# Value block 7 ahead of the scores, four PSUM banks for the last outputs, and a new order for the first tiles of the feed-forward part

## The reference

```python
x = x + tanh(g_xattn) * attention(layernorm(x), ctx, ctx)
x = x + tanh(g_ffn) * ffn(layernorm(x))
```

## Time and profile before

| | us |
|---|---|
| median of 3 runs | 1479.5 |
| the runs | 1479.43 to 1481.12 |
| the profiled execution, its own time | 1474.84 |
| its span in the trace | 1472.9 |

### The profile page before, as it was taken

One profiled execution on the slowest core, in us unless ns is written; L12 is line 12 of the kernel. 1 busy time (PEld: TensorE's weight loads), 2 busy tenths in 40 slices (PEclk: granted clock), 3 DMA queues, 4 the chain that ended last, 5 costly groups with the idle time before them and its releaser, 6 DMA issues.

```text
span 1472.9 us, 19153 instructions
## 1 busy us (share of the span) xinstructions
PE 1424.6 (97%) x7235; PEld 1167.6 (79%) x7248; DVE 1002.9 (68%) x1565; ACT 564.4 (38%) x865; POOL 614.9 (42%) x429
## 2 busy tenths in 40 slices
PE   7999999999999999999999999999999999998887
PEld 7888888888888888887878888888888888874443
DVE  5866675757576766667475757666566667578997
ACT  4424241414142323234542423232232324148995
POOL 3455242434343343441343433434333424243884
PEclk9999999999999999999999999999999999999999
DMA  8834243433425243437265242333343424455565
GB/s 289 264 98 114 78 109 72 109 80 94 102 69 120 65 107 81 104 85 215 95 186 138 68 104 67 92 83 88 86 95 76 106 65 109 85 170 196 129 130 100
DMA packets 327131, 166.52 MB, mean 113 GB/s; under 512 B 275200, under 2 KB 290048, under 8 KB 326656
## 3 DMA queue, kind: packets, MB, share of 16 engines
q1 hardware_dynamic: 324448, 154.29, 39.4%
q0 software_dynamic: 2592, 11.01, 4.5%
HBM read 132.74 MB, written 35.65 MB: 114 GB/s over the span
## 4 chain that ended last, share of the span: by engine, by line
PE 78%; DVE 12%; DMA 3%; issue 2%; POOL 2%; ACT 2%; SPq 1%; POOLq 0%; ACTq 0%; DVEq 0%
PE psum L569 16%; PE psum L571 16%; PE psum L570 16%; PE psum L623 8%; PE psum L658 8%; PE psum L660 7%; PE psum L659 7%; DVE psum L1638 2%; DVE vw_lo L1368 1%; DVE res L1685 1%; DMA acc<-in_x 1%; DMA wv_raw<-in_wv_t 1%; SPq L368 1%; DVE xg L1648 1%; POOL rot L1253 1%
## 5 line engine op out<-in xcount | busy, mean ns | idle before, releaser
L569 PE MATMUL psum<-xt_hi,wq_hi 128*128 128x512 f32 x1024 | 400.9, 391 | 1.5 <-DVE xt_lo L1368 1.5
L571 PE MATMUL psum<-xt_hi,wq_lo 128*128 128x512 f32 x1024 | 398.6, 389 | 0.0
L570 PE MATMUL psum<-xt_lo,wq_hi 128*128 128x512 f32 x1024 | 398.5, 389 | 0.0
L1225 POOL TENSOR_TENSOR wq_lo<-wq_raw,wq_hi 128x512 fp32r<-128x512 f32 x128 | 170.0, 1340 | 484.3 <-ACT wq_hi L932 484.0
L1529 DVE TENSOR_TENSOR acc<-psum,acc 128x512 f32<-128x512 f32 x224 | 151.4, 681 | 140.0 <-PE psum L660 140.0
L1253 POOL TENSOR_TENSOR rot<-rot 128x1024 f32<-128x1024 f32 x64 | 153.6, 2400 | 207.8 <-DVE rot L1472 207.0
L978 ACT ACTIVATE vw_hi<-psum 64x512 fp32r<-64x512 f32 x256 | 151.7, 593 | 191.6 <-PE psum L571 187.9
L569 PEld LDWEIGHTS psum<-xt_hi,wq_hi 128*128 128x128 f32 x1024 | 192.3, 188 | 40.8 <-DVE xt_lo L1368 1.7
L571 PEld LDWEIGHTS psum<-xt_hi,wq_lo 128*128 128x128 f32 x1024 | 192.2, 188 | 40.1
L570 PEld LDWEIGHTS psum<-xt_lo,wq_hi 128*128 128x128 f32 x1024 | 192.4, 188 | 39.2
L1368 DVE TENSOR_TENSOR vw_lo<-psum,vw_hi 64x512 fp32r<-64x512 f32 x256 | 175.5, 687 | 53.9 <-ACT vw_hi L978 47.7
(11 more groups left out here) (153 smaller groups left out, 1910.0 us busy)
## 6 DMA issues: line engine op xcount, KB each, us to landing
wq_raw<-in_wq_t SPq DMA_DIRECT2D x128, 256.0 KB, 4.4
wd_raw<-in_wd_t SPq DMA_DIRECT2D x128, 256.0 KB, 3.7
p_scratch<-prob SPq DMA_DIRECT2D x60, 256.0 KB, 2.0
pt_raw<-p_scratch SPq DMA_DIRECT2D x240, 64.0 KB, 2.5
acc<-in_x SPq DMA_DIRECT2D x16, 512.0 KB, 5.3
out_x<-acc SPq DMA_DIRECT2D x16, 512.0 KB, 4.7
xa<-out_x SPq DMA_DIRECT2D x16, 512.0 KB, 3.6
out_x<-res POOLq DMA_DIRECT2D x15, 512.0 KB, 5.5
```

Of the source, the lines that this page charges most:

```text
L569: pe.matmul(dst, a_hi, b_hi, start=start, stop=False)
L570: pe.matmul(dst, a_hi, b_lo, start=False, stop=False)
L571: return pe.matmul(dst, a_lo, b_hi, start=False, stop=stop)
L1225: pool.tensor_tensor(dst, full, hi.bitcast(F32), ALU.subtract).then_inc(done, 1)
```

## The change

It consists of these parts:

- In `slot` on TensorE, kind 0, filled: `values(gg - 1, 7)` stands ahead of `score(unit - 1)`.
- In the last group of the second half, the outputs from the fifth on use banks 4 to 7 in turn (`out_bank`), on TensorE and in VectorE's `add`. From output 6 on, the wait for adds is for four outputs back; output 6 waits for all `vw_lo`. `gate(0)` and `up(0)` wait for the adds of outputs 12 and 13 (before: 14 and 15), and `turn_inter(0)` waits for all.
- ScalarE's `last_outputs(1)`: `rows(2)` comes between the evacuations of tile 0, `silu(0)` ahead of `evacuate_gate(1)`, one deviation less stands ahead of `evacuate_gate(1)`; the deviations of the last two tiles are done in steps 2 and 3 of the loop.
- VectorE: the copy of the gate's factors stands between the adds of outputs 11 and 12, and tile 2's `scale_gate`, `gate_greatest` and `scales`, with `up_rows(0)` in between, come at the end of `last_outputs(1)`; the loop begins a step later.

```diff
--- before.py
+++ after.py
@@ -318,6 +318,12 @@
                 n, t = c % 2, (c - 2 * BT) // 2
             return b, n, t
 
+        def out_bank(gg, c):
+
+            if gg == HALVES * GROUPS - 1 and c >= 4:
+                return bank(O_BANK + c % 4)
+            return bank(O_BANK + c % 2)
+
         gate_scales = bank(2, 2)[:, P:DIM]
         small_scales = bank(2)[:, 0:16].rearrange("p (k n) -> p k n", k=2)
 
@@ -650,9 +656,14 @@
                     pe.wait_ge(pt_lo_done, gg * UPG + HB + b + 1)
                 if c % BT == 0:
                     pe.wait_ge(vw_lo_done, 2 * (gg * VPG + 4 * ((c // BT) % 2) + 4))
-                if gg * OPG + c >= 2:
+                four = gg == HALVES * GROUPS - 1 and c >= 6
+                if four and c == 6:
+                    pe.wait_ge(vw_lo_done, 2 * (gg * VPG + VPG))
+                if four and c >= 8:
+                    pe.wait_ge(o_done, gg * OPG + c - 3)
+                if not four and gg * OPG + c >= 2:
                     pe.wait_ge(o_done, gg * OPG + c - 1)
-                cols, dst = slice(n * CH, (n + 1) * CH), bank(O_BANK + c % 2)
+                cols, dst = slice(n * CH, (n + 1) * CH), out_bank(gg, c)
                 for p in range(2):
                     p_hi, p_lo = pt_hi[:, p, b, t * P:(t + 1) * P], pt_lo[:, p, b, t * P:(t + 1) * P]
                     pe.matmul(dst, p_hi, vw_hi[:, p, b, cols], start=(p == 0), stop=False)
@@ -670,8 +681,8 @@
                     queries(unit, 2)
                     queries(unit, 3)
                     if filled:
+                        values(gg - 1, 7)
                         score(unit - 1)
-                        values(gg - 1, 7)
                     else:
                         turn_rows(half, 4)
                     queries(unit, 4)
@@ -761,7 +772,7 @@
             def gate(n):
                 if n == 0:
                     pe.wait_ge(fw_in[0], 16)
-                    pe.wait_ge(o_done, HALVES * GROUPS * OPG - 1)
+                    pe.wait_ge(o_done, HALVES * GROUPS * OPG - 3)
                 pe.wait_ge(qg_done, n + 1)
                 if there(n - 1):
                     pe.wait_ge(go_done, n)
@@ -772,7 +783,7 @@
             def up(n):
                 if n == 0:
                     pe.wait_ge(fw_in[1], 16)
-                    pe.wait_ge(o_done, HALVES * GROUPS * OPG)
+                    pe.wait_ge(o_done, HALVES * GROUPS * OPG - 2)
                 pe.wait_ge(qu_done, n + 1)
                 if there(n - 1):
                     pe.wait_ge(uo_done, n)
@@ -809,6 +820,8 @@
 
             def turn_inter(n):
                 pe.wait_ge(ri_done, n + 1)
+                if n == 0:
+                    pe.wait_ge(o_done, HALVES * GROUPS * OPG)
                 if there(n - 1):
                     pe.wait_ge(r_done, n)
                 for c in range(FC):
@@ -1139,16 +1152,15 @@
                     round_rows(0)
                     down_columns()
                     evacuate_gate(0)
+                    rows(2)
                     evacuate_up(0)
                     deviations(1, BT)
                     round_rows(1)
-                    deviations(1, BT + 1)
-                    rows(2)
+                    silu(0)
                     evacuate_gate(1)
-                    silu(0)
                     evacuate_up(1)
                     rows(3)
-                    deviations(1, BT + 2)
+                    deviations(1, BT + 1)
                 if half == 0:
                     copy_rows(1, 1)
                     normalise(3)
@@ -1213,8 +1225,8 @@
                     rows(s + 2)
                 if there(s - 1):
                     silu(s - 1)
-                if s == 3:
-                    deviations(1, HTILES - 1)
+                if s in (2, 3):
+                    deviations(1, HTILES - 4 + s)
                 if s == 4:
                     root(TILES + 2, slice(HTILES, TILES))
 
@@ -1526,10 +1538,10 @@
                 if gg % GROUPS == 0 and n == 0:
                     dve.wait_ge(x_in[tile], 16 * (gg // GROUPS + 1))
                 if gg % GROUPS < GROUPS - 1:
-                    dve.tensor_tensor(acc[:, tile, cols], bank(O_BANK + c % 2), acc[:, tile, cols], ALU.add).then_inc(o_done, 1)
+                    dve.tensor_tensor(acc[:, tile, cols], out_bank(gg, c), acc[:, tile, cols], ALU.add).then_inc(o_done, 1)
                 else:
                     row = gg // GROUPS * HTILES + tile
-                    dve.scalar_tensor_tensor(out=acc[:, tile, cols], in0=bank(O_BANK + c % 2), scalar=1.0, in1=acc[:, tile, cols],
+                    dve.scalar_tensor_tensor(out=acc[:, tile, cols], in0=out_bank(gg, c), scalar=1.0, in1=acc[:, tile, cols],
                                              op0=ALU.mult, op1=ALU.add, accum_out=sums[:, row, n:n + 1]).then_inc(o_done, 1)
 
             def means(tiles, outputs):
@@ -1746,6 +1758,7 @@
                 add(gg - 1, 11)
                 if half == 1:
                     means(slice(HTILES + BT, HTILES + BT + 2), HALVES * GROUPS * OPG - 4)
+                    dve.tensor_copy(gate_scales, v_ig[:, 0:GCOLS]).then_inc(vg_done, 1)
                 add(gg - 1, 12)
                 if half == 0:
                     lower_rows(1, 3)
@@ -1763,7 +1776,10 @@
                 else:
                     means(slice(HTILES + BT + 2, TILES), HALVES * GROUPS * OPG)
                     gate_rows(0)
-                    dve.tensor_copy(gate_scales, v_ig[:, 0:GCOLS]).then_inc(vg_done, 1)
+                    scale_gate(2)
+                    gate_greatest(2)
+                    up_rows(0)
+                    scales(2)
 
             def row_statistics(t):
                 dve.wait_ge(x_in[t], 16)
@@ -1832,8 +1848,8 @@
                         dve.wait_ge(xb_in, 16)
                     dve.tensor_tensor(result(n)[:, cols], result(n)[:, cols], xb[:, cols], ALU.add).then_inc(last_done, 1)
 
-            for s in range(1, TILES + 2):
-                if there(s) and s >= 2:
+            for s in range(2, TILES + 2):
+                if there(s) and s > 2:
                     gate_greatest(s)
                     scales(s)
                 if there(s + 1):
@@ -1847,8 +1863,7 @@
                 if there(s - 3):
                     out_rows(s - 3)
                 if there(s - 1):
-                    if s > 1:
-                        gate_rows(s - 1)
+                    gate_rows(s - 1)
                     up_rows(s - 1)
                 if s == 4:
                     variances(slice(HTILES, TILES), TILES)
```

## The result

| | before | after |
|---|---|---|
| median, us | 1479.47 (4 runs) | 1494.93 (4 runs) |
| the runs | 1478.42 to 1481.12 | 1494.88 to 1497.96 |
| ratio of after to before, with its 95% interval | | 1.0105 (1.0093 to 1.0117) |
| the profiled execution, its own time | 1474.84 | 1494.89 |
| its span | 1472.9 | 1493.1 |

The change costs 15.5 us between the medians, and 20.2 us between the two spans: the profiled execution of the kernel before was 4.6 us under its median, that of the kernel after is at its median. Where these 4.6 us are is shown further on.

What follows compares the result with a forecast made beforehand. TensorE, busy 97% of the span, was taken as the bound, with VectorE to watch behind the last output; 15.8 - 0.6 = +15.2 us gave 1490.0 for the profiled execution, plus 4.7 made 1494.7 us for the median, range 1489 to 1500.

Steps and rivals of the forecast that it cites:

- Part 1: Value block 7 ahead of the scores, 14 places: TensorE waits for POOL's split, 1.13 us each, 15.8 us (14.7 to 17.1).
- Absorption: In the slots: no other wait can shrink to take up the stall, so each place pays its 1.13 us in full.
- the long periods: Three late periods, 2.05 us in excess, where `rot` is late: the split is late too, so the same 1.13 us is added.
- The scores' later end: Scores end 0.78 us later relative to the query parts, delaying ScalarE's and VectorE's steps; costed at nothing.
- the cover in the earlier trace: VectorE's wait of 3.81 us before the next slot's scores, said to cover their later end; without it 0.78 us a place.
- Parts 2 and 3: Tail with four banks and reordered tile steps: 0.6 us won together; bounds 1 us lost to 3.5 us won.
- the wait for `yb`: VectorE's wait of 1.8 us in the tail, to go because ScalarE's normalised rows of tile 2 move up.
- The sign that the prediction named for it: In the profile after, VectorE's distance from the last output's add to the end was to be 0.6 us shorter.
- never idle: VectorE in the tail, behind its longest wait of 1.8 us: said to have no idle time until the last tiles.
- The step to the median: 4.7 us from the profiled execution to the median, added to 1490.0 to give 1494.7 us.
- The rival on the clock: Each new stall brings a lower-clock stretch, 1.7 us a place, 24 us on top: 1518.5 us; chance 3%.
- The rule of the Trainium skill: Cycling PSUM banks with short pauses between matmul groups can swing the clock; by it the time would be 1518.5 us.

Runs made afterwards that it cites:

- Experiment 1: Kernel before with only value block 7 moved ahead of the scores: 1496.68 us; kernel after with that order put back, leaving the tail's changes: 1479.43 us.
- 3: Kernel after with value block 7's weights rounded on ScalarE and split on POOL ahead of the work before them: 1477.18 us, ratio 0.9982.
- 4: Kernel after with only POOL's split moved ahead of its add of `rot`, ScalarE's order left as it was: 1528.66 us, ratio 1.0314.
- 5: Kernel before with the swap in the first half alone: 1488.09 us, repeated 1488.70; kernel before with only the early rounding and split: 1480.42 us.
- before_again: The kernel before, unchanged, run again with a trace of another execution: 1480.23 us.
- keep_busy: early_split with matmuls that nobody reads added in TensorE's waits of the tail: 1469.19 us, ratio to before 0.9929.
- half_swap: Kernel before with value block 7 ahead of the scores in the seven places of the first half alone: 1488.09 us, ratio 1.0058.
- experiment 2: The kernel before, unchanged, run again for a second trace: 1480.23 us over 12 runs.
- swap_only: Kernel before with value block 7 ahead of the scores in its 14 places and nothing else: 1496.68 us, ratio 1.0117.
- pool_only: Kernel after with POOL's split ahead of its add of `rot`, ScalarE's order unchanged: 1528.66 us, ratio 1.0314.
- early_split: Kernel after with value block 7's weights rounded on ScalarE and split on POOL before the work that stood ahead: 1477.18 us, ratio 0.9982.

## Why the prediction was right

Forecast 1494.7 us, measured 1494.93; 15.2 us slower forecast, 15.5 measured. The mechanism that decides, and the direction, were right. That the sum hits within 0.3 us is partly luck: the swap costs about 0.6 us more than its term, and the tail, as far as it can be told, gives back about as much more than its own.

**Part 1, the wait.** The stall was to be 1.10 us and is 1.09 (206.29 to 207.38); the start 0.05 us behind the split's end, and is 0.06; the block 0.79 and is 0.80; the scores 1.70, and are 1.70. By the periods a place costs 1.17 us and not 1.13; some of the pitches behind the scores are 0.24 us where they were 0.23. 14 x 1.17 = 16.4 us instead of 15.8, inside the bounds. Experiment 1 shows that the swap alone costs it, 3 that the weights' split is the cause, 4 that the chain is ScalarE's round, POOL's split, POOL's add, and 5 that it is paid in full at each place.

**Absorption.** None, as said. That the split would be as late in the long periods held in the kernel after too (waits of 1.89 and 1.83 us there, the late `rot` included, against 1.10 in the ordinary ones).

**The scores' later end** was costed at nothing. It is: a period is 1.17 us longer, which the stall explains; the cover in the earlier trace rows was enough.

**Parts 2 and 3** were to give 0.6 us. The steps happened as named: the copy stands before output 12's add, the wait for `yb` is gone, and what is late next is ScalarE and the first `down`. VectorE now waits for that `down` and for the gate and up matmuls behind it, one after the other: 0.98, 0.37 and 0.97 us at 1373.54, 1375.20 and 1376.92, where before it waited 0.93 us for the up matmuls alone. VectorE's waits from 1340 to 1400 us in the kernel after:

```profile
DVE res L1697 <- PE psum L800: 2.0, 2, 1.0
DVE uo L1711 <- PE psum L791: 1.9, 2, 1.0
DVE psum L1650 <- POOL xi L1354: 1.6, 2, 1.0
DVE go L1705 <- PE psum L780: 0.7, 2, 0.4
```

The sign that the prediction named for it did not show: from the start of output 15's add to the end it is 131.0 us in the trace before and 136.8 in the trace after, not 0.6 less, because the two differ by two stretches at the lower clock; against `before_again`, also 136.8, it is nothing. The size stays open between the 0.6 and about 2 us: the direct comparison does not tell it from zero (ratio 1.001, 0.9994 to 1.0025), the traces with equal low stretches give 1.2 us, and those with added matmuls 2.2. All lie inside the bounds. The term says nothing of the clock, which was already down in the rows that it was worked out from: `down` of tile 0 shows 2.82 us for seven of its eight matmuls in the trace before, 3.57 us in that after, and 1.89 for all eight in `keep_busy`. Nor was VectorE "never idle" behind the wait for `yb`, as the prediction has it: besides the 0.93 us it waits 0.80 us for `xi` at 1359.23 and 0.91 for the up matmuls at 1378.67.

**The step to the median.** The prediction took the 4.7 us between the profiled execution and the median as an offset that both kernels share. It held in the medians, but not as meant: the offset goes with two more stretches at the lower clock in the tail, which all later traces without added matmuls but that of `half_swap` have (experiment 2), and the two traces compared with each other give 20 us.

**The rival on the clock** (3%) said that each new stall brings such a stretch. That is false for the kernel after: at its 14 stalls of 1.09 to 1.89 us the scores ran at full clock. Elsewhere the effect exists. At single waits of 1.95, 1.99 and 2.24 us (`swap_only`), and at twelve of 14 pairs of 0.75 and 1.60 us close behind each other (`pool_only`), the clock came down for the scores that followed, at 1.0 to 1.6 us a place. The kernel after stayed clear of it by little, which the prediction could not know. The rule of the Trainium skill weighed there ("TensorE: Matmul & The Clock Gate", "A second HAM failure mode: psum-queue depth-cycling"), that short idle pauses between groups of matmuls can make the clock swing, is borne out by `pool_only`, and not by the kernel after.

## What to carry to other kernels

Before a step is moved ahead on one engine, look up for each of its inputs when it is ready and what stands before it in its maker's own list: here the block's weights were split behind the very add that the block was to hide, and the gain of 0.08 us a period became a loss of 1.17. Move the makers along with the user, all of them, or none. And compare more than one trace of the same kernel before a difference in a stretch with pauses of TensorE is put down to an edit.

## What the hardware showed unexpectedly

The tail of the versions here depends on TensorE's granted clock. Of the 29 runs of the kernel before beside experiments 1 to 3, those at a mean clock of 0.997 took 1471.5 to 1474.7 us and the others 1478.5 and more, with nothing else changed. `down`, eight matmuls of 128x512 in bfloat16, takes 1.9 us or up to 3.6 us, the two levels of 2.4 and 1.2 GHz. 27 added matmuls (8 + 8 + 8 + 3), in waits that stand ahead of such a `down`, took 4.6 us off the kernel before and 8.0 us off `early_split`.

The length of the wait does not decide it alone. The same two waits (0.75 and 1.60 us) brought the clock down at twelve places of one trace and not at two; a `down` ran at full clock behind 2.26 us of idle time and at the lower one behind 2.30. Why the same order of work gets one low stretch in the tail in some executions and three in others is left open. The cause of the three late periods of the kernel before was read but not tried: in one of them VectorE's `pt_lo` takes 1.39 us instead of 0.68 while POOL runs a split that came late, behind a late load.
